# Delta heads of a decoder kernel: the gate projection moved up behind the queries, with the order of banks and weight transposes that goes with it

## The reference, cut to what matters

```python
q = _causal_conv(x @ Wq.T, cw_q, cb_q)
k = _causal_conv(x @ Wk.T, cw_k, cb_k)
v = _causal_conv(x @ Wv.T, cw_v, cb_v)
g = jnp.exp(-jnp.exp(A_log)[None, None, :] * jax.nn.softplus(a + dt_bias[None, None, :]))
beta = jax.nn.sigmoid(b)
q = _l2norm(q.reshape(Bb, Ss, H, DK))
k = _l2norm(k.reshape(Bb, Ss, H, DK))
...
def step(Sstate, inputs):
    q_t, k_t, v_t, g_t, beta_t = inputs
    retrieved = jnp.einsum('bhkv,bhk->bhv', Sstate, k_t)
    error = v_t - g_t[..., None] * retrieved
    update = k_t[..., :, None] * (beta_t[..., None] * error)[..., None, :]
    Snew = g_t[..., None, None] * Sstate + update
    o_t = jnp.einsum('bhkv,bhk->bhv', Snew, q_t)
    return (Snew, o_t)
...
o = o * jax.lax.rsqrt(jnp.mean(o * o, axis=-1, keepdims=True) + EPS) * norm_w
o = o * jax.nn.silu(x @ Wg.T)
return o @ Wo.T
```

## Time and profile before

| what | value |
|---|---|
| median of 3 runs | 3416.99 us (3415.34 to 3425.02) |
| the profiled execution | 3415.16 us |
| its span, first to last instruction | 3413.4 us |
| PE busy | 3180.1 us, 93% |
| PE weight loads | 2544.9 us, 75% |
| DVE busy | 2191.9 us, 64% |
| ACT busy | 1898.9 us, 56% |
| POOL busy | 1672.6 us, 49% |
| mean granted TensorE clock | 0.981 |

### The profile page before, as it was taken

How to read it: one execution, slowest core, us unless ns; L and a number is a source line. 1 busy time by engine, 2 the same in 40 slices (tenths; PEclk the granted TensorE clock), 3 DMA queues, 4 the chain that set the end, 5 groups by cost and what they waited for, 6 DMA issues and landing times. The chain is left out here.

```text
span 3413.4 us, 60026 instructions
## 1 busy us (share of the span) xinstructions
PE 3180.1 (93%) x18834; PEld 2544.9 (75%) x18834; DVE 2191.9 (64%) x4849; ACT 1898.9 (56%) x4657; POOL 1672.6 (49%) x3107
## 2 busy tenths in 40 slices
PE   6899999999999999999999788799979999998998
PEld 3688888888888888888878555488866777776543
DVE  5577777777777777777653488765547567574432
ACT  3677777777777777777532377644445445363111
POOL 2777787777788777778630000145534002011322
PEclk9899999999999999999999999999989999999999
DMA  4222222222222222222353333423351222211854
GB/s 113 63 73 69 59 69 62 73 68 67 74 55 73 62 73 68 65 76 53 97 176 92 115 142 142 177 87 103 115 174 57 68 69 69 93 65 53 271 99 56
DMA packets 432408, 310.47 MB, mean 91 GB/s; under 512 B 130496, under 2 KB 347456, under 8 KB 431072
## 3 DMA queue, kind: packets, MB, share of 16 engines
q1 hardware_dynamic: 423792, 289.57, 28.8%
q0 software_dynamic: 8432, 18.88, 2.8%
HBM read 177.97 MB, written 130.43 MB: 90 GB/s over the span
## 5 line engine op out<-in xcount | busy, mean ns | idle before, releaser
L631 PE MATMUL gd_PJ<-xn_lead,gd_w_rest 128*128 128x512 f32 x1024 | 421.3, 411 | 0.5 <-DVE gd_w_rest L786 0.5
L631 PE MATMUL gd_PJ<-xn_lead,gd_w_lead 128*128 128x512 f32 x1024 | 403.0, 394 | 0.0
L631 PE MATMUL gd_PJ<-xn_rest,gd_w_lead 128*128 128x512 f32 x1024 | 401.9, 393 | 0.0
L1079 POOL TENSOR_TENSOR gd_prod<-gd_L,gd_T 32x14 f32<-32x14 f32 (+6 forms) x896 | 324.8, 362 | 70.4
L1082 POOL TENSOR_TENSOR gd_T<-gd_T,gd_prod 32x14 f32<-32x14 f32 (+6 forms) x896 | 311.6, 348 | 71.6 <-POOL gd_prod L1079 2.5
L793 DVE SCALAR_TENSOR_TENSOR gd_conv<-gd_pre,gd_cur_a,gd_conv 128x512 f32<-128x512 f32 x384 | 301.8, 786 | 13.3 <-ACT gd_conv L958 2.9
L631 PEld LDWEIGHTS gd_PJ<-xn_lead,gd_w_lead 128*128 128x128 f32 x1024 | 193.8, 189 | 43.4
L631 PEld LDWEIGHTS gd_PJ<-xn_lead,gd_w_rest 128*128 128x128 f32 x1024 | 194.4, 190 | 38.5 <-DVE gd_w_rest L786 0.9
L631 PEld LDWEIGHTS gd_PJ<-xn_rest,gd_w_lead 128*128 128x128 f32 x1024 | 194.6, 190 | 35.3
L932 DVE SCALAR_TENSOR_TENSOR gd_og<-gd_B,ptab,gd_gate 128x512 f32<-128x512 f32 x64 | 48.1, 751 | 243.8 <-PE gd_B L645 243.8
L2619 ACT ACTIVATE sa_E<-sa_B,sa_nmax 128x512 f32<-128x512 f32 (+3 forms) x256 | 131.3, 525 | 131.4 <-DVE sa_nmax L2756 127.2
(11 more groups left out here) (476 smaller groups left out, 8620.3 us busy)
## 6 DMA issues: line engine op xcount, KB each, us to landing
expert_rows<-xt_blank SPq DMA_DIRECT2D x16, 2112.0 KB, 7.3
turned_queries_keys<-f_wq SPq DMA_DIRECT2D x16, 1280.0 KB, 6.0
x_wo<-decay_sums SPq DMA_DIRECT2D x64, 256.0 KB, 3.7
triangles<-gd_Lo SPq DMA_DIRECT2D x64, 256.0 KB, 3.5
gd_W<-turned_image SPq DMA_DIRECT2D x64, 256.0 KB
gd_T<-inverse_image SPq DMA_DIRECT2D x64, 256.0 KB
gated_outputs<-gd_og SPq DMA_DIRECT2D x64, 256.0 KB, 2.8
go_ogt<-gated_outputs SPq DMA_DIRECT2D x16, 1024.0 KB, 5.9
```

The lines of the kernel that those rows point to most:

```text
L631: mm = pe.matmul(bank, w_parts[wp][:, j, k, :], rhs, start=(k == 0 and wp == 1), stop=(k == KT - 1 and wp + xp == 0))
L1079: nc.gpsimd.tensor_tensor(prod[:, rows, 0:j], L16[:, rows, j:j + 1].to_broadcast(shape), T16[:, j:j + 1, 0:j].to_broadcast(shape), ALU.mul ...
```

## The change

On **PE** the gate projection is placed directly behind the Q projection, so 24 matmuls stand together between `merge(0)` and `spread_rows(1)`, and the K projection stands alone at the end of the slot. The banks are dealt anew (`W_BANK`): K and G share bank 0, V and Q share bank 1, so that projections that follow each other (K, Q, G, V, K) alternate, and the waits in front of them are changed to fit: Q waits for ACT's copy of V, G for that of K, V for that of Q, K for the SiLU of the gate. The weights are transposed in the order K, G, Q, V (`W_TURN`): K's in slot 1 behind the V projection, G's in slot 2 behind the V projection, Q's in slot 2 in front of the K projection, V's in slot 3 behind the gate projection. `FIRST_BANK` keeps the old banks for head 0.

On **ACT** the SiLU of the gate moves from the end of the slot to behind the copy of Q. On **DVE** the second tap of q moves up to stand with the first, and both now stand in front of the second `Y` (`masked(1)`); the rest parts of the weights are taken at new places. POOL's and SP's programs, the merge levels and all arithmetic are as before.

```diff
         JK, JV, JQ, JG = 0, 1, 2, 3
-        W_BANK = (0, 0, 1, 1)
+        W_BANK = (0, 1, 1, 0)
+        FIRST_BANK = (0, 0, 1, 1)
+        W_TURN = (1, 4, 3, 2)
...
 
-                if back and more and c == CH - 1:
-                    pe.wait_ge(g_silu, n + 2)
-                    turn_weights(h1, JQ)
                 if back:
                     spread_rows(0)
                     if c > 0:
...
                 if has1:
-                    pe.wait_ge(g_silu, n + 2)
-                    pe.wait_ge(w_copied, h1 * 4 + JQ + 1)
+                    if back:
+                        pe.wait_ge(v_pre, n + 3)
+                    pe.wait_ge(w_copied, h1 * 4 + W_TURN[JQ])
                     project(JQ, c1, q_proj)
-                if back and more and c == 1:
-                    pe.wait_ge(k_pre, n + 3)
-                    turn_weights(i + 1, JK)
+                    if has2:
+                        pe.wait_ge(k_pre, n + 3)
+                    elif back:
+                        pe.wait_ge(g_silu, n + 2)
+                    pe.wait_ge(w_copied, h1 * 4 + W_TURN[JG])
+                    project(JG, c1, g_proj)
+                if back and more and c == CH - 1:
+                    pe.wait_ge(q_pre, n + 2)
+                    turn_weights(h1, JV)
...
-                if back and more and c == CH - 1:
+                if has1:
                     pe.wait_ge(q_pre, n + 2)
-                    turn_weights(h1, JG)
-                if has1:
-                    if has2:
-                        pe.wait_ge(k_pre, n + 3)
-                    else:
-                        pe.wait_ge(v_pre, n + 3)
-                    if back and more and c == 1:
-                        pe.wait_ge(w_copied, (i + 1) * 4 + JK + 1)
-                    else:
-                        pe.wait_ge(w_copied, h1 * 4 + JV + 1)
+                    pe.wait_ge(w_copied, h1 * 4 + W_TURN[JV])
                     project(JV, c1, v_proj)
...
                     each(Bk[1], tiles(Kd), tiles(U), s_sum)
-                if back and more and c == 2:
-                    pe.wait_ge(v_pre, n + 4)
-                    turn_weights(i + 1, JV)
                 if has1:
                     pe.wait_ge(q_len, n + 2)
                     turned(Bk[5], k_m, k_turned)
-                    pe.wait_ge(q_pre, n + 2)
-                    pe.wait_ge(w_copied, h1 * 4 + JG + 1)
-                    project(JG, c1, g_proj)
+                if back and more and c == 2:
+                    pe.wait_ge(v_pre, n + 4)
+                    turn_weights(i + 1, JQ)
                 if has3:
-                    pe.wait_ge(v_pre, n + 4)
+                    if has1:
+                        pe.wait_ge(g_silu, n + 3)
                     if not back:
                         pe.wait_ge(w_copied, 4)
                     elif c == 2:
-                        pe.wait_ge(w_copied, (i + 1) * 4 + JV + 1)
+                        pe.wait_ge(w_copied, (i + 1) * 4 + W_TURN[JG])
                     else:
-                        pe.wait_ge(w_copied, h3 * 4 + JK + 1)
...
                 if back:
                     pe.wait_ge(o_ready, n + 2)
                     turned(Bk[0], tiles(o), o_turned)
 
-            turn_weights(0, JK)
-            turn_weights(0, JQ)
...
                     turned_blocks()
-                    masked(1)
                 if has1:
                     dve.wait_ge(q_halo, n + 2)
                     dve.wait_ge(q_pre, n + 2)
-                    tap(n + 1, parm, PQ, cur_a, (0,), q_tap)
-                if back and more and c == 1:
-                    rest_weights(i + 1, JK)
+                    tap(n + 1, parm, PQ, cur_a, (0, 1), q_tap)
+                if back:
+                    masked(1)
+                if back and more and c == CH - 1:
...
                     st.then_inc(lo_ready, 1)
-                if back and more and c == CH - 1:
-                    rest_weights(h1, JG)
+                if back and more and c in (1, 2):
+                    rest_weights(i + 1, JK if c == 1 else JG)
...
                     act.wait_ge(head_a, h1 + 1)
                     copy_pre(parm, PQ, JQ, cur_a, q_pre)
-                if back and more and c == 1:
-                    lead_weights(i + 1, JK)
+                    act.wait_ge(g_proj, n + 2)
+                    if back:
+                        act.wait_ge(og_ready, n + 1)
+                    nc.scalar.activation(gate[:, parm, :], PJ[:, W_BANK[JG], :], ACT.Silu).then_inc(g_silu, 1)
+                if back and more and c == CH - 1:
+                    lead_weights(h1, JV)
...
                     silu(PQ, qT[:, parm, :], q_silu)
-                if back and more and c == CH - 1:
-                    lead_weights(h1, JG)
                 if has1:
                     act.wait_ge(v_proj, n + 2)
                     copy_pre(parm, PV, JV, cur_a, v_pre)
+                if back and more and c in (1, 2):
+                    lead_weights(i + 1, JK if c == 1 else JG)
...
                     nc.scalar.activation(DT[:, (c + 3) % CH], above[:, parm], ACT.Exp).then_inc(d_exp, 1)
-                if has1:
-                    act.wait_ge(g_proj, n + 2)
-                    nc.scalar.activation(gate[:, parm, :], PJ[:, W_BANK[JG], :], ACT.Silu).then_inc(g_silu, 1)
+                if back and more and c == 2:
+                    lead_weights(i + 1, JQ)
```

More of the change, by code:

```diff
@@ L618, in _, with turn_weights @@
         def _(pe):
-            def turn_weights(h, j):
+            def turn_weights(h, j, banks=W_BANK):
                 pe.wait_ge(w_in, h * 64 + 64)
                 for k in range(KT):
-                    tr = pe.transpose(PJ[:, W_BANK[j], k * P:(k + 1) * P], wraw[:, j, k * P:(k + 1) * P], ident)
+                    tr = pe.transpose(PJ[:, banks[j], k * P:(k + 1) * P], wraw[:, j, k * P:(k + 1) * P], ident)
                 tr.then_inc(w_turned, 1)
@@ L769, in slot @@
                     turned(Bk[0], tiles(o), o_turned)
-            turn_weights(0, JK)
-            turn_weights(0, JQ)
+            turn_weights(0, JK, FIRST_BANK)
+            turn_weights(0, JQ, FIRST_BANK)
             pe.wait_ge(w_copied, 1)
@@ L775, in _ @@
             pe.wait_ge(w_copied, 2)
-            turn_weights(0, JG)
+            turn_weights(0, JG, FIRST_BANK)
             pe.wait_ge(k_pre, 1)
-            turn_weights(0, JV)
+            turn_weights(0, JV, FIRST_BANK)
             slots(pe, slot, 2)
@@ L782, in _, with rest_weights @@
         def _(dve):
-            def rest_weights(h, j, n=None):
-                dve.wait_ge(w_lead, h * 4 + (j if n is None else n) + 1)
+            def rest_weights(h, j, n=None, banks=W_BANK):
+                dve.wait_ge(w_lead, h * 4 + (W_TURN[j] if n is None else n + 1))
                 lead, rest = (part[:, j].rearrange("p k n -> p (k n)") for part in w_parts)
-                nc.vector.tensor_tensor(rest, PJ[:, W_BANK[j], :], lead.bitcast(F32), ALU.subtract).then_inc(w_copied, 1)
+                nc.vector.tensor_tensor(rest, PJ[:, banks[j], :], lead.bitcast(F32), ALU.subtract).then_inc(w_copied, 1)
             def tap(m, parm, j, cur, ds, done):
@@ L872, in slot @@
                 if has1:
-                    tap(n + 1, parm, PQ, cur_a, (1, 2), q_tap)
+                    tap(n + 1, parm, PQ, cur_a, (2,), q_tap)
                 if has2:
@@ L920, in slot @@
                         nc.vector.tensor_copy(S[:], Bk[1][:, :, :]).then_inc(s_ready, 1)
-                if back and more and c == 2:
-                    rest_weights(i + 1, JV)
                 if has1:
@@ L949, in _, with lead_weights @@
         def _(act):
-            def lead_weights(h, j, n=None):
-                act.wait_ge(w_turned, h * 4 + (j if n is None else n) + 1)
-                nc.scalar.copy(w_parts[0][:, j].rearrange("p k n -> p (k n)"), PJ[:, W_BANK[j], :]).then_inc(w_lead, 1)
+            def lead_weights(h, j, n=None, banks=W_BANK):
+                act.wait_ge(w_turned, h * 4 + (W_TURN[j] if n is None else n + 1))
+                nc.scalar.copy(w_parts[0][:, j].rearrange("p k n -> p (k n)"), PJ[:, banks[j], :]).then_inc(w_lead, 1)
             def copy_pre(parm, j, w, cur, done):
@@ L1018, in slot @@
                     silu(PV, vT[:, :], v_silu)
-                if back and more and c == 2:
-                    lead_weights(i + 1, JV)
                 if has3:
@@ L1041, in _ @@
             act.sem_inc(g_silu, 1)
-            lead_weights(0, JK, 0)
-            lead_weights(0, JQ, 1)
+            lead_weights(0, JK, 0, FIRST_BANK)
+            lead_weights(0, JQ, 1, FIRST_BANK)
             act.wait_ge(head_k, 1)
@@ L1046, in _ @@
             copy_pre(0, PK, JK, cur_k, k_pre)
-            lead_weights(0, JG, 2)
-            lead_weights(0, JV, 3)
+            lead_weights(0, JG, 2, FIRST_BANK)
+            lead_weights(0, JV, 3, FIRST_BANK)
             slots(act, slot)
```

13 lines of the change are left out of this document (8 added, 5 removed).

## The result

The change runs in **3493.18 us** (median of 4 runs, 3487.73 to 3494.04), the kernel before in 3416.16 us (4 runs, 3413.04 to 3425.02): ratio 1.0218, 95% interval 1.0196 to 1.024. The forecast was 3460, with a range that ended at 3490; the median lies 3 us beyond that end. Direction and chain are as forecast; the size is 33 us short. The profiled execution took 3494.04 us, with a span of 3492.2.

The account below looks back on a forecast made before the run. PE was taken to lead, with POOL's chain from slot 3's V projection to slot 1 equally long to within 0.7 us. The sum was 3415.2 + 34 (chain) + 10 (slot 2) = 3459, stated as 3460 us, range 3432 to 3490.

Parts of the forecast that it names:

- The chain across the turn: Slot 3's V projection through q_max, POOL's pause and solve to slot 1's spread: 2.45 us later, 14 times, 34 us.
- The late copy of Q's weights: Slot 3's start: ACT's copy and DVE's rest part come late for Q, 0.3 us a turn within the 2.45.
- Slot 2's wait: PE stands 0.9 us before merge(1) for the second Y where it stood 0.2: 15 x 0.7 = 10 us.
- The rest at nothing: Weight transposes, ACT's table loads, K's wait for the gate's SiLU, starts of slots 2, 3 and 0: no cost.
- The delay eats more: Rival: G waits for K's copy in slot 2, V slips again; about 1 us in 56 slots, 3516 us; chance 0.10.
- The pause swallows it: Rival: POOL's 2.72 us pause before L1098 absorbs the late q_max; only slot 2's 10 us paid, 3425 us; chance 0.06.
- Faster: Rival: all of PE's 21.8 us of waits go and POOL's solve sheds over 2.5 us; 3393 us; chance 0.04.

Follow-up runs that it names:

- Moving the factors: The change, with POOL's wait for q_max and the three operations behind it moved behind the next slot's decay arguments: 3454.74 us.
- kernel with 3-head turns: The change, with POOL's loop of 15 heads written as 5 turns of 3 heads: 3447.81 us.
- the early mask: The change, with DVE's masked(1), which writes the second Y, put back ahead of the two taps of q: 3478.77 us.

## Why the prediction fell short, and what in it was right

- **The chain across the turn was right in mechanism and low in size.** Forecast, from slot 3's start to slot 1's: 14 x 2.45 = 34 us, a DMA wait near 3 us, `q_max` near 21 us, the pause unchanged. Measured: 43 us, or 3.05 a turn, with waits of 2.8 us, `q_max` at 21.3, a pause of 2.74. Moving the factors removes the wait, cutting the turns removes it where no turn is left. Of the 0.6 us that a turn is over the forecast, the decay arguments beside the taps of k are 0.6 (booked at nothing), Q's weights 0.25, the pause 0.15 and the DMAs 0.1, and the solve gives 0.5 back.
- **The late copy of Q's weights was in the right place, at about half its size.** It was booked at 0.3 us a turn. PE waits 0.33 us for it in slot 3, 15 times, and starts Q 3.55 us behind the slot's start where it started at 3.03: 0.5 us, by which `q_max` is later too. Taken away in the kernel with 3-head turns, where the chain binds at four turns only, it gives 7.4 us (379.9 to 372.5).
- **Slot 2's wait was right in kind and path, low in size.** Forecast 15 x 0.7 = 10, measured 14, with a wait of 1.13 us where 0.9 was said. It needs both causes that the forecast names, GpSimd's lateness and DVE's new order. With `Y` ahead of the taps slot 2 to slot 3 falls from 421.2 to 405.6 us (the wait for `W` then costs slot 3 to slot 0 another 12 us), and with the factors moved it falls to 402.2 under the new order.
- **The step that failed is "The rest at nothing".** It took PE's standing as the whole price of a stand. The forecast read a clock of 1.00 in the earlier trace rows and did not ask what it rested on: no stand in the head stage over 0.9 us. With 2.8 us, 10 heads of 14 paid 1.63 or 2.75 us more, 20 us in all. With it the forecast's own sum is 3459 + 20 = 3479, inside the range; with 4 more in slot 2 and 9 in the chain it is 3492.
- **The rivals.** "The delay eats more" did not come: PE's list has no wait in front of G, and the periods of the other slots don't grow from head to head. "The pause swallows it" is refuted by the 3-head turns. The Trainium skill (Advanced Engine Details and Errata, Control Flow Timing) gives about 108 ns for a compare-and-branch. The traces differ: 2.7 us at each of these turns, 14 or 4 times as the loop is written. "Faster" did not come by itself, but the same order with the factors moved and Q's weights early gives 3398.59, near the 3393 that this rival worked out from PE alone.

Open: why 4 of the 14 heads keep the full clock behind the same stand, and what the pause consists of. The length of the stand does not decide by itself: with the early mask the clock fell behind stands of 1.7 and 1.9 us and stayed behind one of 2.7. The trace has a packet of instructions fetched within a microsecond of POOL's last instruction at each of the turns; that it is the cause was not tried. Whether the gain of 3398.59 over before belongs to the order of the projections is not settled either: the kernel before with 3-head turns reaches 3401.31, and their ranges overlap. The order of the kernel before, with one tap of q between the second `Y` and the merged `W`, was not tried in the change.

## What to carry to other kernels

When a change makes the leading engine stand longer, price the stand and then the slower clock behind it: here PE's wait for the DMA grew by 31 us in all, and the half clock behind it cost another 20. Where two engines work in step, ask for a moved piece of work not only who waits for it but who works beside it; a pause can be worth more than the work that fills it. And a wait that vanishes has not been won until the list of waits as a whole is shorter: in four of these ten kernels (the early mask twice, the moved factors twice) one wait went and another came elsewhere.

## What the runs showed of the hardware

- TensorE's granted clock fell to half (1.2 GHz) for 3.4 or 6.8 us behind stands of 2.6 to 3.2 us in the change (10 of 14 heads, with 6.8 us behind the three longest), of 2.0 us with the factors moved (13 of 15), and of 1.7 to 2.6 us with the early mask (4 of 14, while stands of 2.4 and 2.7 us kept the full clock); never in the head stage behind the stands of up to 1.2 us in slot 2 or slot 0. Adding 2.7 us of useless matmuls a head into the stand made the kernel 19 us faster.
- GpSimd pauses 2.7 us at a turn of its loop here, and the pause goes with the turns: 14 to 4 of them, 45 us of the change's time and 15 to 19 of the kernel before's.
- Three taps of VectorE over 128x512 take 2.31 us alone and 4.72 beside GpSimd's operations over 128x512. The Trainium skill (GPSIMD Engine Reference, Key points) says that the two share SBUF interfaces; the trace agrees, with a factor of 2.0 for this pair. The GpSimd operations stretch less: the second of the three takes 1.60 us instead of 1.30.
